# A memset behind each indirect move of rows on GpSimd

## The reference

```python
x = x + 0.5 * ffn(layernorm(x))
x = x + attention(layernorm(x))
x = x + 0.5 * ffn(layernorm(x))

def ffn(x):
    shared = (silu(x @ shared_gate.T) * (x @ shared_up.T)) @ shared_down.T
    probs = sigmoid(x @ router_w.T + routing_bias)          # 8 experts
    scores, indices = top_k(probs, 2)
    scores = scores / sum(scores)
    w = zeros(tokens, 8); w[token, indices] += scores
    g = silu(x @ gate_w[e]); u = x @ up_w[e]                # for each expert e, 256 wide
    return shared + sum over e of w[:, e] * ((g * u) @ down_w[e])

def attention(x):                                           # 8 heads of 16
    q, k, v, gate = x @ Wq.T, x @ Wk.T, x @ Wv.T, x @ Wg.T
    q, k = rope(q), rope(k)
    o = (q @ (k.T @ v) * scale + sum(v)) / (q @ sum(k) * scale + 512)
    return ((o + depthwise_conv(v)) * gate) @ Wo.T
```

## Time and profile before

| | us |
|---|---|
| median of the runs (not traced) | 479.21 |
| span of the profiled execution, first to last instruction | 501.9 |
| TensorE busy in it | 462.0 (92%) |
| VectorE busy | 346.8 (69%) |
| GpSimd busy | 282.3 (56%) |
| ScalarE busy | 271.0 (54%) |

### The profile page before, as it was taken

One profiled execution on the slowest core, in us unless ns is written; L12 is line 12 of the kernel. 1 busy time (PEld: TensorE's weight loads), 2 busy tenths in 40 slices (PEclk: granted clock), 3 DMA queues, 4 the chain that ended last, 5 costly groups with the idle time before them and its releaser, 6 DMA issues.

```text
span 501.9 us, 9741 instructions
## 1 busy us (share of the span) xinstructions
PE 462.0 (92%) x2975; PEld 382.8 (76%) x2975; DVE 346.8 (69%) x1064; ACT 271.0 (54%) x612; POOL 282.3 (56%) x290
## 2 busy tenths in 40 slices
PE   8979899989899999899989998999998998999896
PEld 4868678877788787688767877877776777888776
DVE  4999993333568865868889898899876532454355
ACT  5936135555476555476546664655464555565421
POOL 4148556665567245566636655686654555666562
PEclk9999999999999999999989999999999999999999
DMA  8981233253421334321132322114342253543323
GB/s 237 370 283 39 68 107 116 80 167 113 111 73 64 101 80 116 92 68 57 54 102 56 91 75 74 43 39 123 88 128 84 78 163 105 150 113 104 86 73 106
DMA packets 74353, 53.68 MB, mean 107 GB/s; under 512 B 9664, under 2 KB 68928, under 8 KB 74304
## 3 DMA queue, kind: packets, MB, share of 16 engines
q1 hardware_dynamic: 66112, 36.26, 24.4%
q0 software_dynamic: 8192, 16.79, 11.0%
HBM read 26.87 MB, written 26.15 MB: 106 GB/s over the span
## 4 chain that ended last, share of the span: by engine, by line
PE 50%; DVE 26%; issue 10%; ACT 6%; another core or an unknown queue 5%; DMA 2%; POOL 0%; SPq 0%; DVEq 0%; ACTq 0%; POOLq 0%
PE pool L888 12%; PE pool L877 6%; PE gu L843 5%; PE gu L845 5%; PE gu L844 5%; DVE X L1242 3%; PE gu L804 2%; DVE hs L1219 2%; PE pool L826 2%; DVE hs L1223 2%; PE gu L802 2%; DVE raw L1421 2%; PE gu L803 2%; DVE stats L1253 2%
## 5 line engine op out<-in xcount | busy, mean ns | idle before, releaser
L1176 POOL DMA_INDIRECT yg<-y_sorted,places x128 | 124.2, 970 | 94.3 <-PE gu L845 42.0
L1156 POOL DMA_INDIRECT x_sorted<-xn,places x128 | 129.7, 1013 | 83.3 <-PE gu L845 30.8
L1219 DVE TENSOR_TENSOR hs<-gs,gu 128x512 f32<-128x512 f32 x92 | 60.7, 663 | 89.4 <-ACT gs L1033 64.7
L1033 ACT ACTIVATE gs<-gu 128x512 f32<-128x512 f32 x124 | 72.1, 583 | 70.8 <-PE gu L804 24.8
L888 PE MATMUL pool<-w,hT 128*128 x708 | 99.3, 283 | 11.6 <-ACT hT L1039 9.7
L888 PEld LDWEIGHTS pool<-w,hT 128*128 128x128 f32 x708 | 87.6, 191 | 26.4 <-issue 23.0
L843 PE MATMUL gu<-w,xbt_hi 128*128 x177 | 81.8, 462 | 1.8 <-DVE xbt_lo L1205 1.5
L1039 ACT ACTIVATE hT<-pool 128x512 f32<-128x512 f32 x92 | 53.3, 580 | 36.2 <-PE pool L877 24.8
L845 PE MATMUL gu<-w,xbt_hi 128*128 x177 | 70.0, 396 | 0.0
L844 PE MATMUL gu<-w,xbt_lo 128*128 x177 | 69.9, 395 | 0.0
L1014 ACT ACTIVATE ys<-pool 128x256 f32<-128x256 f32 x92 | 34.5, 376 | 62.6 <-PE pool L888 34.2
(11 more groups left out here) (132 smaller groups left out, 786.8 us busy)
## 6 DMA issues: line engine op xcount, KB each, us to landing
xb<-x_sorted SPq DMA_DIRECT2D x85, 128.0 KB
y_sorted<-ys SPq DMA_DIRECT2D x85, 128.0 KB
x_sorted<-yg SPq DMA_DIRECT2D x6, 512.0 KB, 6.3
X<-x_dram SPq DMA_DIRECT2D x8, 256.0 KB, 4.8
x_sorted<-xn,places POOLq DMA_INDIRECT x128
yg<-y_sorted,places POOLq DMA_INDIRECT x128
out_dram<-X SPq DMA_DIRECT2D x8, 256.0 KB
raw<-gate_w_dram SPq DMA_DIRECT2D x4, 256.0 KB, 4.8
```

The source lines that it names most:

```text
L1033: nc.scalar.activation(dst, src, ACT.Silu).then_inc(silu_done, 1)
L1156: nc.gpsimd.indirect_dma_start(x_sorted[g], bass.IndirectOffsetOnAxis(places[g][:, k, t:t + 1], 0), xn[:, b, t % T], None).then_inc(scatte ...
L1176: nc.gpsimd.indirect_dma_start(yg[slot][:, k, t], None, y_sorted[g], bass.IndirectOffsetOnAxis(places[g][:, k, at:at + 1], 0)).then_inc(ga ...
L1219: v.tensor_tensor(hs[n % HB][:].rearrange("p (j i) -> p j i", j=2)[:, 0:k], gs[n % GB][:].rearrange("p (j i) -> p j i", j=2)[:, 0:k], bank ...
```

## The change

Behind each scatter and each gather GpSimd writes zeros to a region of 128 partitions x 384 bytes (`spare`, in the triangle of `squares_sb` that is dead by then). Each of these memsets waits for the one before it (semaphore `parted`), and ahead of GpSimd's list stands one more wait, for `earlier_done`, so that the triangle has been read. The order of the list and the waits of `pace` are as they were, and the plan is the same.

```diff
--- before.py
+++ after.py
@@ -1,4 +1,5 @@
 from contextlib import ExitStack
+from itertools import count as counter
 
 import numpy as np
 import concourse.bass as bass
@@ -12,6 +13,7 @@
 F32R = mybir.dt.float32r
 BF16 = mybir.dt.bfloat16
 I32 = mybir.dt.int32
+U8 = mybir.dt.uint8
 
 B, S, D = 8, 512, 128
 T = S // P
@@ -37,6 +39,7 @@
 HOP_PE, ADDRESS = 20, 11
 LOADED, COLD = 4, 340
 WARM = 20
+PARTED = 384
 LETTERS = "".join(chr(c) for c in range(35, 126) if c not in (39, 92))
 URGENCY = (
     "WLFWSb^ukX}PPPnPCcJNT;RELRIJR8=6@K?didXL<:VH0&UF>CSFKJaSYsKdP]JRNN5L3reTK/]YP[UOTFBVLWXSmQM{YMeWcIMPVu]/PKNPLU"
@@ -572,6 +575,7 @@
         ve, rstd = sb("ve", [P, 4, B, T]), sb("rstd", [P, 4, B, T])
         shifts = sb("shifts", [P, 4, B, T])
         minus_half = sb("minus_half", [P, T])
+        spare = squares_sb[:, 1].bitcast(U8)[:, 0:PARTED]
 
         groups = range(NG)
         wsel = [sb(f"wsel{g}", [P, 2, tiles(g)]) for g in groups]
@@ -665,7 +669,7 @@
         rden_done, widened, rbc_ready, rbc_done = (sem(n) for n in ("rden_done", "widened", "rbc_ready", "rbc_done"))
         conv0_done, conv_link, num_ready, att_done = sem("conv0_done"), sem("conv_link"), sem("num_ready"), sem("att_done")
         o_sum_done, oT_done, proj_ready = sem("o_sum_done"), sem("oT_done"), sem("proj_ready")
-        stored = sem("stored")
+        stored, parted = sem("stored"), sem("parted")
 
         def wait(eng, s, value):
             if value > 0:
@@ -1143,6 +1147,13 @@
                 wait(once, half_ready, half_through)
                 wait(once, gu_ready, through)
 
+            parts = counter()
+
+            def part_moves():
+
+                wait(once, parted, next(parts))
+                nc.gpsimd.memset(spare, 0).then_inc(parted, 1)
+
             def scatter(g, n):
                 t, k = n // 2, n % 2
                 l, b = GROUPS[g][t // T]
@@ -1156,6 +1167,7 @@
                 nc.gpsimd.indirect_dma_start(
                     x_sorted[g], bass.IndirectOffsetOnAxis(places[g][:, k, t:t + 1], 0),
                     xn[:, b, t % T], None).then_inc(scattered[g], 16)
+                part_moves()
 
             def gather(l, b, n):
                 g = group_of(l, b)
@@ -1184,6 +1197,7 @@
             nc.gpsimd.memset(vT[1][:], 0.0)
             nc.gpsimd.memset(v_tok[:], 1.0).then_inc(pads_set, 1)
             once.wait_ge(half_set, 1)
+            once.wait_ge(earlier_done, 1)
 
             run("POOL", {"root": root, "scatter": scatter, "gather": gather})
```

## The result

The changed kernel takes **497.06 us** (median; 495.45 to 500.24), against 479.33 us (477.92 to 480.57) for the kernel before beside it: 1.037 times as long, 95% interval 1.032 to 1.042. The forecast was 470.1 us, with a range up to 485.5: wrong in sign, and outside the range. Of the 44 runs of the kernel before that stand beside the experiments one took 894.0 us; no trace of it is kept, and the ratios leave it out.

What follows compares the result with a forecast made beforehand. TensorE, half of the chain, was taken to stall on its late signals behind runs of GpSimd moves. Gain -12.9 plus loss 3.8 made -9.1 us, taken off the 479.2 us median: 470.1 us, range 462.0 to 485.5.

Steps and rivals of the forecast that it cites:

- Moves that follow at once make TensorE's finished work known late: GpSimd's runs of moves under 0.4 us apart: TensorE's signals come late, ending when GpSimd pauses; ys starts 2.5 us late.
- I take the difference over as it is: From traced span to runs: the sum of -9.1 us, applied unchanged to the runs' median of 479.2 us, gives 470.1.
- the 22.7 us between span and runs: The kernel before: median of the runs, 479.2 us, against the traced span of 501.9 us.
- the 25 us of nameless chain: Chain that ended last: 5%, some 25 us, under another core or an unknown queue; set beside the tracing rival.
- the gain term: TensorE's idle time behind runs of moves, ahead of L888, L877 and L843, goes: 12.9 us, bounds 0 to 16.3.
- The handover: GpSimd, move to move: 0.96 + 0.42 (memset) + 0.20 (gap) = 1.58 us instead of 1.26; bounds 1.34 and 1.75.
- Loss 3.8 us, bounds 0 to 14.7: Last moves of groups and batches come later, 0.32 us per handover adding up within a run: 3.8 us together.
- POOL becomes the bound: Rival: 256 handovers and 18 roots fill GpSimd's time, deciding from 1.64 us each; 485.5 us at 1.70; chance 0.17.
- the hold belongs to the tracing: Rival: late signals exist only when traced, so the span falls but the runs don't; 479 to 483 us; chance 0.23.
- Wrong if POOL has hardly an idle time left and PE waits for xb or yg: Sign in the changed kernel's trace, with the runs still at 479 us or not stated: GpSimd would be the bound.
- small tensor_scalar instructions of VectorE that a region could block: Shared port of GpSimd and VectorE: memsets block some of 24 adds for up to 0.42 us; 2 us at most.

Runs made afterwards that it cites:

- the second trace: The kernel before, unchanged, traced once more: runs 479.46 us (ratio 0.999, 0.997 to 1.001), traced span 477.3 us.

## Why the prediction was wrong, point by point

**"Moves that follow at once make TensorE's finished work known late": right for the trace that was read, wrong as a cause.** In that execution the two stood together 116 times, and never behind two spacings of 1.5 us or more in a row. In the kernel without pace waits 214 of 255 spacings are under 1.45 us, against 129 in that trace, and no signal is late. So more than the moves was needed; what, that one execution doesn't show.

**"I take the difference over as it is": the step that failed.** The traced sum met its own target to 1.2 us (492.8 against 494.0), but only because both its terms were too small: the disturbance was worth 501.9 - 477.3 = 24.6 us, not 12.9, and the loss in the spans 16.7, not 3.8. That the sum fitted is luck. And the 22.7 us between span and runs were not a fixed cost of tracing: in all later executions the difference is 1.8 to 2.0 us with the other sign, the run above the span. The 22.7 us agree with the disturbance (24.6, against the second trace), and so do the 25 us of nameless chain that I put beside them in the rival and didn't draw the consequence from. So the gain term, 12.9 us, measures next to 0: in the second trace, before any change, TensorE's idle time for hT is 0.3 us, and the waits for hs and xbt_lo are 3.3 and 0.5, of which the forecast left 3.2 and 0.2 standing.

**The handover: right.** The region takes 0.435 us (0.42 forecast), so it goes by elements and not by bytes; the gap behind it is 0.165 to 0.17 us (0.20), behind the move none. Moves start 1.57 us apart in a run (1.58).

**"Loss 3.8 us, bounds 0 to 14.7": mis-sized, 17.6 us measured in the stretch of the moves.** I priced late moves at the ends of runs one by one, as if each run began on time. Without idle time between the runs each begins late by what the one before it lost. The lag of the changed kernel behind the second trace of the kernel before, by the start of the same move: -0.5 us at the first (32.7 against 33.3), 6.5 at the 113th move (235.4 against 228.9), 14.8 at the 177th (359.0 against 344.2), 17.1 at the end of the last (486.03 against 468.96). Nearly half of it (8.3 us) comes in from 229 to 344 us of the kernel before, where the changed kernel's moves and roots have four pauses of over 0.35 us between them, and those of the kernel before over twenty.

**The rival "POOL becomes the bound" was the right one, with the wrong point.** It divided all of 438.6 - 18.7 us by 256 moves, 1.64 us each, and saw that 1.58 fits. The stretch itself was well estimated (435.7). But the sum left out the waits that no pace can remove. In the changed kernel 26.5 us of idle time lie in gaps over 0.35 us, 22.3 with 512 elements: waits for variances, for rows of y and for places, the rows shown above. Taking 22 us off gives (438.6 - 18.7 - 22) / 256 = 1.55 us, under the 1.58 forecast. The cost also begins before the limit, because the cushion isn't where it is needed: at 288 elements, with 40.9 us left in such gaps, 6.4 us were already lost (487.00 against 480.59 beside it). The mean handover measured, 1.59 us ((257.6 + 111.0 + 40.5 - 1.4 of overlap) / 256), was on the wrong side.

**The rival "the hold belongs to the tracing"** named the right consequence (nothing to gain). Its reason is half refuted: eleven further executions were traced too, four of them of kernels with no region, and none has a late signal, so tracing alone doesn't do it. But the first record lacks nearly half of the semaphore updates, so a disturbance by the recording of that one execution isn't ruled out.

**"Wrong if POOL has hardly an idle time left and PE waits for xb or yg": half seen.** GpSimd is as told, but TensorE's wait for xb is only 3.1 us; VectorE's adds wait 8.5 us for gathered rows (2.3 in the second trace), and its shifts 10.9 us for roots that stand behind moves on GpSimd (1.6):

```profile
DVE shifts L1281 <- POOL rstd L1142: 10.9, 10, 2.0
DVE X L1256 <- DMA yg<-y_sorted,places: 8.5, 6, 1.9
```

The root was in the prediction only as GpSimd's time, never as somebody's data: the one instruction queued behind the moves whose waiting reader I didn't name.

## What to carry to other kernels

When the span of the trace is 5% off the timed runs, settle first where the difference sits: here it was in the very waits that the change was to remove, and they weren't there in the runs. Landing times that stand in one page and are missing in another of the same kernel were a second sign. An engine at 56% busy isn't free: take its own data waits off its idle time, and what is left, the time that it waits for others' pace, is the cushion that longer instructions use up; the cost sets in before it is gone. And a pattern that appears a hundred times in one trace is still one execution; two traces would have shown it here.

## What the runs showed of the hardware

A memset on GpSimd of 192, 288, 384 and 512 one-byte elements a partition takes 275, 355, 435 and 542 ns: 0.83 ns an element, with some 0.115 us beside. That gives 0.22 and 0.54 us for the 2-byte and 4-byte regions of the earlier trace rows (0.20 and 0.53 there), so by these rows the type doesn't matter.

The prediction left 2 us at most (2.3 by its own factors) out of its sum for small tensor_scalar instructions of VectorE that a region could block. They did get slower, and by more: all 82 by 7.0 us (15.8 to 22.8), the 24 of ve from 178 ns in the second trace of the kernel before to 263, 24 x 0.085 = 2.0 us, and the eight of ks_bd from 225 to 437. The means hide that most stay as they were: 17 of the 24 of ve take 169 to 218 ns, the other seven 308 to 652.

```profile
L1263 DVE TENSOR_SCALAR ve<-mv 128x4 f32<-128x4 f32 x24 | 4.3, 178 | 0.8
...
L1463 DVE TENSOR_SCALAR ks_bd<-hmask,pool 128x8 f32<-128x8 f32 x8 | 1.8, 225 | 0.0
```

```profile
L1277 DVE TENSOR_SCALAR ve<-mv 128x4 f32<-128x4 f32 x24 | 6.3, 263 | 0.9
...
L1477 DVE TENSOR_SCALAR ks_bd<-hmask,pool 128x8 f32<-128x8 f32 x8 | 3.5, 437 | 0.0
```

Products of two tensors don't change: the 85 of hs, one input of which (gu) lies in PSUM, take 681 and 682 ns, and six of found (128x64, both inputs in SBUF) 230 and 226. That is the Trainium skill's rule (SBUF — State Buffer, Who interferes with whom): a tensor_scalar in a two-port mode and a GpSimd instruction block one another, while a tensor_tensor isn't held up by a GpSimd instruction that only writes. This case's traces agree on both halves, as far as these rows go (on the second by found, since hs has only one input in SBUF); which mode the instructions ran in no row shows.

That a single traced execution can hold TensorE's signals back by up to 3.4 us, 116 of them by over 0.2 us, stays without a cause here.
